# A decoder block with routed experts: bias rows added by VectorE from tables instead of bias products on TensorE

## The reference

```python
def _L0_ffn_ref(input, Wg, W1, b1, W2, b2):      # E = 8 experts, D = 256, H = 512, TOP_K = 2
    logits = jnp.einsum('bsd,de->bse', input, Wg)
    probs = jax.nn.softmax(logits, axis=-1)
    top_vals, top_idx = jax.lax.top_k(probs, TOP_K)
    top_vals = top_vals / jnp.sum(top_vals, axis=-1, keepdims=True)
    onehot = jax.nn.one_hot(top_idx, E, dtype=input.dtype)
    mask, scores = jnp.sum(onehot, axis=2), jnp.sum(onehot * top_vals[..., None], axis=2)
    xm = input[None] * jnp.moveaxis(mask, -1, 0)[..., None]
    h = jax.nn.relu(jnp.einsum('ebsd,edh->ebsh', xm, W1) + b1[:, None, None, :])
    y = jnp.einsum('ebsh,ehd->ebsd', h, W2) + b2[:, None, None, :]
    return jnp.sum(y * jnp.moveaxis(scores, -1, 0)[..., None], axis=0)
```

## Time and profile before

| | us |
|---|---|
| median of 3 executions | 1969.67 (1967.25 to 1970.55) |
| the profiled execution | 1963.07 |
| its span, first to last instruction | 1961.3 |
| TensorE busy, matmul | 1737.8 (89%) |
| TensorE busy, weight loads | 1217.5 (62%) |
| GpSimd busy | 1262.2 (64%) |
| VectorE busy | 1148.2 (59%) |
| ScalarE busy | 864.6 (44%) |

### The profile page before, as it was taken

How to read it: one execution, slowest core, us unless ns; L and a number is a source line. 1 busy time by engine, 2 the same in 40 slices (tenths; PEclk the granted TensorE clock), 3 DMA queues, 4 the chain that set the end, 5 groups by cost and what they waited for, 6 DMA issues and landing times. The chain is left out here.

```text
span 1961.3 us, 32756 instructions
## 1 busy us (share of the span) xinstructions
PE 1737.8 (89%) x10682; PEld 1217.5 (62%) x10682; DVE 1148.2 (59%) x2005; ACT 864.6 (44%) x1280; POOL 1262.2 (64%) x709
## 2 busy tenths in 40 slices
PE   6654499999989999998999999989999999649992
PEld 4544366666656666666666666656666666337991
DVE  4776465556565656666555656565666555663444
ACT  3222234444444444454444444444444444324443
POOL 3875438677686676776867667676677686236554
PEclk8877699999999999999999999999999999759996
DMA  6001300000100000010000000200000000033224
GB/s 191 4 22 38 113 1 23 1 23 0 68 10 23 1 24 22 1 55 22 22 1 23 2 22 0 77 1 22 15 9 23 3 14 1 22 103 109 69 71 139
DMA packets 38853, 68.09 MB, mean 35 GB/s; under 512 B 4600, under 2 KB 28544, under 8 KB 37696
## 3 DMA queue, kind: packets, MB, share of 16 engines
q1 hardware_dynamic: 34976, 56.12, 8.6%
q0 software_dynamic: 3744, 10.23, 1.7%
HBM read 52.84 MB, written 13.50 MB: 34 GB/s over the span
## 5 line engine op out<-in xcount | busy, mean ns | idle before, releaser
L1034 POOL TENSOR_TENSOR xa_total<-xa_total,xa_pexp 128x1024 f32<-128x1024 f32 (+1 forms) x341 | 832.4, 2441 | 61.9 <-ACT xa_pexp L975 38.3
L1107 DVE TENSOR_REDUCE xa_parts<-ps_ring 128x1 f32<-128x402 f32 x1024 | 532.4, 566 | 267.1 <-PE ps_ring L920 253.9
L975 ACT ACTIVATE xa_pexp<-ps_s 128x1024 f32<-128x1024 f32 (+1 forms) x416 | 426.2, 1026 | 399.1 <-PE ps_s L875 360.2
L889 PE MATMUL ps_pv<-xa_pexp,xa_v 128*64 128x512 f32 (+1 forms) x1664 | 399.7, 604 | 0.0
L920 PE MATMUL ps_ring<-xa_k_hi,xa_q_hi 64*128 64x402 f32 x1024 | 245.1, 376 | 7.4 <-DVE xa_parts L1107 5.0
L889 PEld LDWEIGHTS ps_pv<-xa_pexp,xa_v 128*64 128x64 f32 (+1 forms) x1664 | 106.1, 136 | 181.0 <-issue 142.6
L875 PE MATMUL ps_s<-xa_q_hi,xa_k_hi 64*128 64x512 f32 (+1 forms) x832 | 203.1, 437 | 3.3 <-DVE xa_k_lo L1095 1.4
L1095 DVE TENSOR_TENSOR xa_k_lo<-ps_ring,xa_k_hi 128x402 fp32r<-128x402 f32 (+1 forms) x128 | 73.7, 576 | 218.7 <-ACT xa_k_hi L986 218.7
L920 PEld LDWEIGHTS ps_ring<-xa_k_hi,xa_q_hi 64*128 64x128 f32 x1024 | 149.7, 185 | 78.8 <-issue 23.1
L875 PE MATMUL ps_s<-xa_q_neg,xa_row_one 64*128 64x512 f32 (+1 forms) x832 | 180.4, 393 | 0.0
L875 PE MATMUL ps_s<-xa_q_lo,xa_k_hi 64*128 64x512 f32 (+1 forms) x832 | 179.8, 392 | 0.0
(11 more groups left out here) (274 smaller groups left out, 2965.3 us busy)
## 6 DMA issues: line engine op xcount, KB each, us to landing
wa_raw<-in_pack_a SPq DMA_DIRECT2D x17, 768.0 KB, 4.4
ex_raw<-in_pack_e SPq DMA_DIRECT2D x8, 1024.0 KB, 5.8
ctx_raw<-in_ctxT SPq DMA_DIRECT2D x4, 1601.0 KB, 8.6
wb_raw<-in_pack_b SPq DMA_DIRECT2D x16, 256.0 KB, 2.6
ex_w_hi<-ybuf SPq DMA_DIRECT2D x8, 512.0 KB, 8.1
sa_xT<-in_xT SPq DMA_DIRECT2D x8, 256.0 KB, 6.2
X<-in_x SPq DMA_DIRECT2D x1, 2048.0 KB, 11.8
x_hi<-sa_x1s_hi SPq DMA_DIRECT2D x16, 128.0 KB, 2.1
```

What stands on the lines that cost most here:

```text
L889: ins = nc.tensor.matmul(ps_pv[half(h), :], v[0:m, t, at:at + XD], pexp[0:m, buf, h, :], start=t == 0, stop=t == MT - 1)
L975: nc.scalar.activation(pexp[0:m, buf], ps_s[0:m, (p * MT + t) % 2], ACT.Exp, scale=XD ** -0.5)\
L1034: engine.tensor_tensor(total[p][0:m], first, pexp[0:m, buf], ALU.add).then_inc(s["add_done"], 1)
L1107: nc.vector.tensor_reduce(parts[:, h, q, c:c + 1], ps_ring[:, r, 0:CW], AX.X, ALU.max)\
```

## The change

The two bias products per block, `sel`, `pick` and `bx` go. Two tables hold the bias rows of all experts on every partition: `b1_all` (128 x 8 x 512) and `b2_all` (128 x 8 x 256). VectorE reads the block's expert into a register of its own and adds the row `b1_all[e]` while it takes h out of PSUM (that was ScalarE's copy), and the row `b2_all[e]` while it takes y out. `b2_all` is loaded by one broadcast transfer at the start of `experts`. b1 is turned by TensorE at the start of `experts` and copied out by VectorE behind its statistics; SyncE stores the eight rows to memory and loads them back as a broadcast.

To make room, `xb_hi`, `xb_lo`, `h_f`, `h_hi` and `h_lo` have one place instead of two, the arrays of the list share their room with these, and `one_r` is half as large and is filled a second time behind the products that read it. Layer two starts when the high part of h is there and waits for the low part before its last four products.

```diff
 # Ahead: b2_raw and its load go
+        self.b1_rows = nc.dram_tensor("b1_rows", [1, NE * HID], F32, kind="Internal").ap()
 # experts, arrays
-        bx = sb("bx", [P, HID + E], F32R)
+        b1_all, b2_all = sb("b1_all", [P, NE, HID]), sb("b2_all", [P, NE, E])
-        xb_hi, xb_lo = sb("xb_hi", [P, 2, E], F32R), sb("xb_lo", [P, 2, E], F32R)
-        sel = sb("sel", [P, 2, P], F32R)
+        xb_hi, xb_lo = sb("xb_hi", [P, E], F32R), sb("xb_lo", [P, E], F32R)
+        h_f, h_hi, h_lo = sb("h_f", [P, HID]), sb("h_hi", [P, HID], F32R), sb("h_lo", [P, HID], F32R)
+            one_r = tmp("one_r", [P, ASG // 2, P], BF16)
 # SyncE, ahead of the x2 stores
+            sp.dma_start(b2_all[:].rearrange("p e n -> p (e n)"),
+                         a["b2"].rearrange("(o e) n -> o (e n)", o=1).broadcast_to([P, NE * E])).then_inc(s["b2_in"], 16)
+            sp.wait_ge(s["b1_turned"], 1)
+            sp.dma_start(ahead.b1_rows.rearrange("o (e n) -> (o e) n", e=NE), b1_row[:]).then_inc(s["b1_out"], 16)
+            sp.wait_ge(s["b1_out"], 16)
+            sp.dma_start(b1_all[:].rearrange("p e n -> p (e n)"), ahead.b1_rows.broadcast_to([P, NE * HID]))\
+                .then_inc(s["b1_in"], 16)
 # TensorE: the four turns of b1c move from behind the list's products to the program's start
-                pe.wait_ge(s["sel_done"], q + 1)
-                nc.tensor.matmul(ps_h[:, q % 2, :], sel[:, q % 2], bx[:, 0:HID], start=False, stop=True)\
-                    .then_inc(s["h_mm"], 1)
 ...
-                pe.wait_ge(s["h_done"], q + 1)
+                pe.wait_ge(s["h_hi_done"], q + 1)
                 need(pe, s["y_copied"], q - 1)
-                nc.tensor.matmul(ps_y[:, q % 2, 0:E], sel[:, q % 2], bx[:, HID:HID + E], start=True, stop=False)
                 terms = [(h, w, c) for h, w in ((h_hi, w_hi), (h_hi, w_lo), (h_lo, w_hi)) for c in range(HC)]
                 for n, (h, w, c) in enumerate(terms):
+                    if n == 2 * HC:
+                        pe.wait_ge(s["h_done"], q + 1)
 # ScalarE: take_h and the making of sel and bx go
 # VectorE
+            dve.wait_ge(s["b1_tr"], 1)
+            nc.vector.tensor_copy(b1_row[:], ps_y[0:NE, 1, :]).then_inc(s["b1_turned"], 1)
 ...
-            nc.vector.tensor_tensor(bx[LO:LO + NE, 0:HID], ps_y[0:NE, 1, :], bx[0:NE, 0:HID].bitcast(F32),
-                                    ALU.subtract).then_inc(s["b_ready"], 1)
 ...
+            def take_h(q):
+                e = dve.value_load(eidi[0:1, q:q + 1], min_val=0, max_val=NE - 1)
+                experts_of[q] = e
+                dve.wait_ge(s["h_mm"], q + 1)
+                need(dve, s["h_tr"], q)
+                nc.vector.tensor_tensor(h_f[:], ps_h[:, q % 2],
+                                        b1_all[:, bass.ds(e, 1), :].rearrange("p a n -> p (a n)"), ALU.add)\
+                    .then_inc(s["h_copied"], 1)
 # take_y
-                nc.vector.tensor_copy(y_sb[:, q % 3], ps_y[:, q % 2, 0:E]).then_inc(s["y_copied"], 1)
+                nc.vector.tensor_tensor(y_sb[:, q % 3], ps_y[:, q % 2, 0:E],
+                                        b2_all[:, bass.ds(experts_of[q], 1), :].rearrange("p a n -> p (a n)"), ALU.add)\
+                    .then_inc(s["y_copied"], 1)
+            dve.wait_ge(s["b1_in"], 16)
             take_x(0)
             for q in range(NBK):
+                take_h(q)
                 if q + 1 < NBK:
                     take_x(q + 1)
```

More of the change, by code:

```diff
@@ L1197, in experts @@
-        steps16 = sb("steps16", [P, NE, T])
-        blocks, ends = sb("blocks", [P, NE]), sb("ends", [P, NE])
-        place = sb("place", [P, T, NE])
-        picked = sb("picked", [P, TOPK, T, NE])
-        pos, quo, rem = sb("pos", [P, ASG]), sb("quo", [P, ASG]), sb("rem", [P, ASG])
-        iota = sb("iota", [P, P])
-        iota_a = sb("iota_a", [P, ASG])
-        col = sb("col", [P, 1])
-        row_of, second = sb("row_of", [P, 1]), sb("second", [P, 1])
-        spare = sb("spare", [P, NBK])
@@ L1222, in experts, with tmp @@
-        h_hi, h_lo = sb("h_hi", [P, 2, HID], F32R), sb("h_lo", [P, 2, HID], F32R)
-        h_f, y_sb = sb("h_f", [P, 2, HID]), sb("y_sb", [P, 3, E])
+        norm = sb("norm", [P, T, TOPK])
+        gidx, sidx = sb("gidx", [P, NBK], U32), sb("sidx", [P, NBK], U32)
+        eidi = sb("eidi", [P, NBK], U32)
+        with ExitStack() as short:
+            def tmp(name, shape, dt=F32):
+                return short.enter_context(nc.sbuf_tensor("ex_" + name, shape, dt))
+            probs = tmp("probs", [P, T, NE])
+            gred = tmp("gred", [P, T])
+            top = tmp("top", [P, T, 8])
+            idx = tmp("idx", [P, T, 8], U32)
+            idxf = tmp("idxf", [P, T, 8])
+            hot = tmp("hot", [P, TOPK, T, NE])
+            mask = tmp("mask", [P, T, NE])
+            below = tmp("below", [P, P])
+            run = tmp("run", [P, NE, T])
+            tot = tmp("tot", [P, NE, T])
+            before_e = tmp("before_e", [P, NE])
+            count = tmp("count", [P, NE])
+            steps16 = tmp("steps16", [P, NE, T])
+            blocks, ends = tmp("blocks", [P, NE]), tmp("ends", [P, NE])
+            place = tmp("place", [P, T, NE])
+            picked = tmp("picked", [P, TOPK, T, NE])
+            pos, quo, rem = tmp("pos", [P, ASG]), tmp("quo", [P, ASG]), tmp("rem", [P, ASG])
+            iota = tmp("iota", [P, P])
+            iota_a = tmp("iota_a", [P, ASG])
+            col = tmp("col", [P, 1])
+            spare = tmp("spare", [P, NBK])
+            full, wrap, pad = tmp("full", [P, NBK]), tmp("wrap", [P, NBK]), tmp("pad", [P, NBK])
+            eid = tmp("eid", [P, NBK])
+            one_r = tmp("one_r", [P, ASG // 2, P], BF16)
+            with ExitStack() as late:
+                past = late.enter_context(nc.sbuf_tensor("ex_past", [P, NBK, NE], F32))
+            one_q = tmp("one_q", [P, ASG, NBK], BF16)
+            with ExitStack() as gate_only:
+                xT_f = gate_only.enter_context(nc.sbuf_tensor("ex_xT_f", [P, 2, EC, P], F32))
+                b1_row = gate_only.enter_context(nc.sbuf_tensor("ex_b1_row", [NE, HID], F32))
+            val_q = tmp("val_q", [P, ASG, 2, NBK], BF16)
@@ L1361, in _ @@
         def _(pe):
-            pe.wait_ge(ahead.sems["small_in"], 48)
+            pe.wait_ge(ahead.sems["small_in"], 32)
+            for c in range(HC):
+                ins = nc.tensor.transpose(ps_y[0:NE, 1, c * P:(c + 1) * P], b1c[:, :, c], ident[:])
+            ins.then_inc(s["b1_tr"], 1)
             def gate(t):
@@ L1390, in _ @@
                         pe.wait_ge(s["val_done"], 2)
-                ins = nc.tensor.matmul(ps_y[:, 0, 0:2 * NBK], one_r[:, n], val_q[:, n].rearrange("p a q -> p (a q)"),
+                ins = nc.tensor.matmul(ps_y[:, 0, 0:2 * NBK], one_r[:, n % 16], val_q[:, n].rearrange("p a q -> p (a q)"),
                                        start=n == 0, stop=n == ASG - 1)
-            ins.then_inc(s["table_mm"], 1)
-            for c in range(HC):
-                ins = nc.tensor.transpose(ps_y[0:NE, 1, c * P:(c + 1) * P], b1c[:, :, c], ident[:])
-            ins.then_inc(s["b1_tr"], 1)
+                if n % 8 == 7:
+                    ins.then_inc(s["table_step"], 1)
             def turn_x(q):
@@ L1426, in turn_h @@
                 for c in range(HC):
[L1427 removed]
+                    ins = nc.tensor.transpose(ps_t[:, q % 2, c * P:(c + 1) * P], h_f[:, c * P:(c + 1) * P], ident[:])
                 ins.then_inc(s["h_tr"], 1)
@@ L1456, in _ @@
         def _(act):
-            act.wait_ge(s["zero_set"], 1)
-            nc.scalar.copy(bx[:], zero[:, 0:1].broadcast_to([P, HID + E]))
             def take_weights(e):
```

96 lines of the change are left out of this document (29 added, 67 removed).

## The result

The changed kernel took 1960.9 us (median of 9 executions, 1959.0 to 1965.0), the kernel before 1967.5 beside it (9 executions, 1966.6 to 1971.5): a ratio of 0.9974, 95% interval 0.9965 to 0.9982, which is 3.5 to 6.9 us. 1956.4 was forecast, with 13.3 us of gain; the medians lie 6.6 apart, and the ratio makes it 5.1.

A forecast was written before the change was run, and what follows sets the result against it. TensorE's issue slots were taken to bound the block loop. Steady blocks -11.85, loop ends -1.4, blocks 0 to 7 with bias preparation -1.1 and loads +1.1 gave -13.3, so 1956.4 us from 1969.67; range 1953.0 to 1964.0.

The forecast's parts named there:

- Bias products gone: Block loop: slots of 0.23 and 0.20 leave TensorE, taking a block from 3.795 to 3.365 if nothing else becomes late.
- TensorE's load chain: Block loop: TensorE's register load of the expert number, behind the wait for h, costs 0 to 0.20 a block, taken 0.035.
- h copied by VectorE: Block loop: the copy becomes an addition of 0.69 with a bias row; h ready at 1.02, wanted at 1.55, so covered.
- VectorE's register load: Block loop: new expert number load once a block, some 0.6, free if it runs while the low part of h is computed.
- rivals 1 and 2: VectorE's register load in the block loop: not hidden, 3.70 a block, 1965.4 (12%); or twice as long, 1960.0 (5%).
- Single buffers: Block loop: one place instead of two for tokens, h and their parts adds waits for steps already passed, so 0.
- Ends of the loop: First and last blocks: bias slots gone and the last layer two starting on the high part of h, together -1.4.
- blocks 0 to 7: First blocks wait for gathers queued on GpSimd; less work on TensorE there gives -0.8, an estimate.
- On VectorE the bias preparation ahead of the first tokens goes: Between list and first tokens: 0.68 for the longer of two pieces, counted as 0.3 since the tokens' arrival limits it too.
- Loads: SyncE's table transfers ahead of the x2 stores delay expert 2's weights, the gate's exponential and the list: +1.1, bounds 0 and +4.3.
- Rival 3: Start of the expert part: the broadcast is slow, 2 MB taking 10.5 instead of 5.2, +5.3, 1961.7; chance 13%.
- Rival 4: Same broadcast, far worse: over 22 us for 2 MB, list 18.3 late, kernel over 0.2% slower; chance 3%.

The follow-up runs named there:

- r4: Kernel before without its two bias products per block, layer two starting on the high part of h: 1954.6 us, ratio 0.9955.
- r5: Changed kernel with TensorE's and VectorE's loads of the next expert number moved ahead of their waits for h: 1954.9 us, ratio 0.9956.
- r14: Changed kernel with both engines' expert numbers loaded early, the same kernel as r5, run beside r12: 1955.6 us, ratio to the kernel before 0.9959.
- r0: Changed kernel unedited, run again for a second profile: 1959.8 us, ratio to the kernel before 0.9980.
- r2: Kernel before without its two bias products per block, nothing else changed, output lacking both biases: 1962.1 us, ratio 0.9991.
- r12: Changed kernel unedited, profiled again as the base for three runs on the same chip: 1957.6 us, ratio to the kernel before 0.9972.
- r3: Kernel before with VectorE forming expert 3's low weights ahead of the bias table, nothing removed: 1966.7 us, ratio 1.0018.
- r1: Changed kernel with expert 5's weight load issued only when the first gather has landed: 1956.9 us, ratio to the kernel before 0.9969.
- r7: Changed kernel with VectorE's low halves moved behind first gather's issue and first tokens, numbers early, broadcasts behind expert 2's weights: 1953.3 us, ratio 0.9951.
- r9: Changed kernel with GpSimd's low half of expert 2's weights held until VectorE has scaled the gate's probabilities: 1958.9 us, ratio 0.9951.

## Why the prediction was off

**Bias products gone, 3.365 at best: wrong size.** A removed product gives back what the next one doesn't take over. Of the 0.20 of layer two's bias slot, 0.09 is the change from turning to wide products; r4 shows it without any of the other edits. 3.795 - 0.23 - 0.12 = 3.45; measured 3.46. The slots are 0.095 a block dearer than my 3.365, 2.85 in 30 blocks.

**TensorE's load chain, 0 to 0.20, taken 0.035: the size fits, the mechanism only in part.** I had it in every block. In nine of ten it costs nothing, and the tenth is some 0.3 longer because VectorE's addition starts late; r5 and r14, which move both engines' loads, take 0.87 off 30 blocks, where I had about 1.05. Loop: -9.2 instead of -11.85, which is 2.85 for the slots less 0.2 here.

**h copied by VectorE: right.** 0.69, begun 0.31 after layer one. **VectorE's register load, rivals 1 and 2: rejected.** 39 loads on VectorE took 0.303 at the median in the first profile. They run while the low part of h is computed (in r0 from 1841.09, the low part from 1841.07), and no block of 3.46 waited for them. Whether they have a part in the long blocks is open.

**Single buffers, y with its bias, GpSimd's and ScalarE's work: right**, each 0. Layer two's start on the high part was booked as 0.7 at the end only. r2 and r4 show that in the kernel before it is worth 0.16 in each block once the bias products are gone (3.63 against 3.47). The changed kernel without it was not run.

**Ends of the loop -1.4, blocks 0 to 7 -0.8: right in r12** (-1.6, -1.0); in r0 the blocks up to 8 took 1.1 more than before, so the second is within what varies by itself.

**"On VectorE the bias preparation ahead of the first tokens goes ... I count 0.3": the step that failed.** Beyond these 0.3 the sum takes the wait from the list to the first tokens as unchanged, without a reason, and it grew by 4.2 to 4.5. I asked only whether VectorE's queue would be shorter. It became so, and what stood behind it, two low halves of weights, moved ahead of GpSimd's first gather. That lengthened the gather instruction by 1.15 and let a 1 MB load go out in front of its transfer, another 3.3. r3 makes that loss in the kernel before; r1 takes the transfer's part of it away and r7 both. It is the largest error of the sum.

**Loads +1.1: the size fits, the path was another.** The list was late by 0.5 to 2.3 (0.5 in r12, 1.4 in the first profile, 2.3 in r0). I had it run over the exponential. It runs over GpSimd's low half of the same weights, which holds VectorE up (r9). The 16 KB, for which I had estimated 3, were through in 1.5. **Rival 3**, a slow broadcast that costs 5.3, is rejected: the broadcast landed 8.5 after its issue, beside the stores, where I had 5.2 and the rival 10.5, and the list was some 0.7 late, 2.3 at most. **Rival 4** needed 18 of lateness.

Together: -13.3, +2.7 in the loop, +4.2 at the first tokens, -0.6 at the list, -0.3 in the rest gives -7.3 for the profile of r12 (-7.2 in the table, by rounding); the medians measured beside it differ by 5.3. The measured 1960.9 lies in the range of 1953 to 1964, but not for a reason that I had named: that is luck. The base helped, too: 1969.67 was the median of three executions, and nine gave 1967.5.

## What to carry to other kernels

When work is removed from an engine, follow what moves up behind it on that engine, and ask what that now runs ahead of: a buffer freed 1 us sooner sent a 1 MB load in front of a small gather that everything waited for. Before a slot is counted as gained, ask which wait it had covered and which cost the next instruction takes over; a run with only the removal (r2) tells both. Where an operation of 16 K elements takes 3 or 4 us, look at what the engine beside it ran at that time.
